# Expert stages of an attention and mixture-of-experts block: three programs merged into one, 128-row blocks, weights split once and streamed

## The reference

```python
mod = (silu(c) @ wmod).reshape(4, 6, 1, 512)           # sa, ca, ga, sb, cb, gb
h = layernorm(x) * (1 + ca) + sa
x = x + ga * attention(h)                              # 16 heads, causal, compressed keys and values
h = layernorm(x) * (1 + cb) + sb
aff = sigmoid(h @ wa)                                  # 16 experts
p, i = top_k(aff, 2); p = p / sum(p)
expert(h) = (gelu(h @ g + gb) * (h @ w1 + b1)) @ w2 + b2      # 512 -> 256 -> 512
routed = sum over the two chosen experts of p * expert(h)
shared = sum over 2 shared experts of expert(h)
out = x + gb * (h + shared + routed)
```

## Time and profile before

| | us |
|---|---|
| median of 3 timed runs | 1675.2 (1673.89 to 1675.54) |
| profiled execution | 1671.57 |
| its span, first to last instruction | 1669.7 |

### The profile page before, as it was taken

How to read it: one execution, slowest core, us unless ns; L and a number is a source line. 1 busy time by engine, 2 the same in 40 slices (tenths; PEclk the granted TensorE clock), 3 DMA queues, 4 the chain that set the end, 5 groups by cost and what they waited for, 6 DMA issues and landing times. The chain is left out here.

```text
span 1669.7 us, 26373 instructions
## 1 busy us (share of the span) xinstructions
PE 1475.5 (88%) x8146; PEld 1241.6 (74%) x8146; DVE 1006.6 (60%) x2079; ACT 613.9 (37%) x1281; POOL 491.5 (29%) x281
## 2 busy tenths in 40 slices
PE   6858892999999999989999899479994999999974
PEld 4436672888888888878888788357773999999931
DVE  3566661666668766686667766344355666666647
ACT  2332221444433434434444334121211556565510
POOL 0005574100007300380005600252001555545435
PEclk9969996999999999999999999879997999999965
DMA  9876777522242322423222420150003788889746
GB/s 305 287 207 216 218 215 251 210 70 64 69 160 80 137 75 63 157 95 125 69 76 68 157 72 30 64 196 26 26 0 99 232 288 280 286 275 281 237 146 194
DMA packets 138425, 254.91 MB, mean 153 GB/s; under 512 B 22844, under 2 KB 68832, under 8 KB 136836
## 3 DMA queue, kind: packets, MB, share of 16 engines
q1 hardware_dynamic: 123000, 191.84, 36.1%
q0 software_dynamic: 15376, 62.46, 11.1%
HBM read 186.00 MB, written 68.21 MB: 152 GB/s over the span
## 5 line engine op out<-in xcount | busy, mean ns | idle before, releaser
L897 ACT ACTIVATE a_pr<-a_pr,a_nmax 128x128 f32<-128x128 f32 (+3 forms) x256 | 142.2, 556 | 120.5 <-DVE a_nmax L949 120.0
L1631 POOL DMA_INDIRECT e_xg<-h_d,e_idx x64 | 75.7, 1183 | 274.0 <-DVE e_idx L1732 264.0
L96 PE MATMUL e_pg<-e_xT,e_w 128*128 128x256 f32 x512 | 145.2, 284 | 4.7 <-POOL e_w L1637 2.7
L97 PE MATMUL e_pg<-e_xT,e_w 128*128 128x256 f32 x512 | 144.9, 283 | 0.0
L98 PE MATMUL e_pg<-e_xT,e_w 128*128 128x256 f32 x512 | 144.7, 283 | 0.0
L949 DVE CUSTOM_DVE_ANT_0 a_pr<-a_psS,a_mask 128x128 f32<-128x128 f32 (+3 forms) x256 | 115.7, 486 | 38.2 <-PE a_psS L1027 37.1
L1039 PE MATMUL a_psY<-a_pT,a_cv 128*128 128x256 f32 (+2 forms) x768 | 134.5, 325 | 1.9 <-DVE a_pT L971 1.9
L1039 PEld LDWEIGHTS a_psY<-a_pT,a_cv 128*128 128x128 f32 x768 | 125.2, 189 | 14.6 <-issue 2.1
L96 PE MATMUL a_psX<-a_hT,a_wqk 128*128 (+1 forms) x256 | 100.7, 394 | 28.9 <-POOLq L855 28.9
L957 DVE TENSOR_SCALAR a_pr<-a_pr,a_rinv 128x128 f32<-128x128 f32 (+3 forms) x256 | 123.6, 546 | 2.2
L848 POOL DMA_DIRECT2D a_cv<-c_d x4 | 2.2, 538 | 405.2 <-PE a_psY L1039 405.2
(11 more groups left out here) (270 smaller groups left out, 3956.2 us busy)
## 6 DMA issues: line engine op xcount, KB each, us to landing
a_wqk<-wqk_d SPq DMA_DIRECT2D x64, 512.0 KB, 3.4
e_st<-in_L_ffn_rw SPq DMA_DIRECT2D x64, 512.0 KB
qpe_d<-p_qs SPq DMA_DIRECT2D x64, 256.0 KB, 4.3
a_qpe<-qpe_d SPq DMA_DIRECT2D x64, 256.0 KB, 2.6
e_st<-in_L_ffn_rg SPq DMA_DIRECT2D x32, 512.0 KB
y_d<-e_yo SPq DMA_DIRECT2D x32, 512.0 KB, 6.4
wqk_d<-w_hl SPq DMA_DIRECT2D x16, 512.0 KB, 5.4
hT_d<-p_hT SPq DMA_DIRECT2D x4, 2048.0 KB, 8.6
```

Source lines behind the costliest of these rows:

```text
L96: nc.tensor.matmul(out, sh, mh, start=n == 0, stop=False)
L97: nc.tensor.matmul(out, sh, ml, start=False, stop=False)
L897: nc.scalar.activation(pr[i], pr[i], ACT.Exp, bias=nmax[:, i:i + 1], scale=-1.0, accum_out=rsum[:, i:i + 1]).then_inc(ex, 1)
L1631: pool.indirect_dma_start(out=xg[:, u, i], out_offset=None, in_=K.h2_d, in_offset=bass.IndirectOffsetOnAxis(ap=idx[:, u, i:i + 1], axis=0) ...
```

## The change

**Blocks.** `PB` is 128 instead of 256, and there are 47 blocks instead of 32. In a block the rows are the stationary operand and the weights move: gate and up of 256 columns each are one group of 12 matmuls of 128x512, the second product 6 of 128x512, and each group gets one more matmul that adds the biases, by a one-hot of the block's expert. The product y2 then has rows on partitions and is transposed twice for the second product.

**Weights.** The routed and shared experts' weights are split once, in 72 pieces, during attention: SP loads a raw piece (three DMAs, 384 KB), ScalarE copies it (`split_high`), VectorE subtracts (`split_low`), SP stores both parts to w1s_d and w2s_d. Heads 0 to 7 carry two pieces each, the others one. In the expert stage GpSimd's queue loads 2 MB + 1 MB of split weights once per expert into a ring of three slots; TensorE reads expert and slot of each block into registers.

**Rows.** h of the second norm is spread to xs_d, in the order of the places, by 32 indirect stores; blocks then load 128 rows directly. xs_d is filled with zeros (12 DMAs of GpSimd's queue, 12.3 MB) at the beginning of attention, as places without a token are read too.

**Mhl** isn't kept: `stage_weights` stores its two parts (16 x 512 KB) to mhl_d, and attention loads 1 MB of it for each pair of heads.

**One program.** `stage_shared`, `stage_routed` and `stage_combine` become `stage_ffn`, with no barrier inside. Its order on TensorE: shared experts of sequences 0, 1, 2, then the 47 blocks, then the shared experts of sequence 3. The gathers and the combination run beside that last sequence. The sums of sequences 0 to 2 go through sum_d.

The diff, cut to its core (lines of a deleted function stand only where the text needs them):

```diff
-PB = 2 * P
-NBLK = (B * S * TOP) // PB + E
+PB = P
+NBLK = (B * S * TOP - E) // PB + E
...
 # stage_weights
-                        nc.scalar.activation(Mhl[:, bass.ds(h, 1), 0, :].rearrange("p a n -> p (a n)"),
-                                             pm[:, u % 2], ACT.Copy).then_inc(hi_w, 1)
+                        nc.scalar.activation(ml[:, u, 0], pm[:, u % 2], ACT.Copy).then_inc(hi_w, 1)
...
+                        sp.dma_start(K.mhl_d[bass.ds(j * (NI // 2) + u // 2, 1), :, u % 2].rearrange("a p s n -> (a p) s n"),
+                                     ml[:, u].bitcast(F32)).then_inc(out_s[u], 16)
...
 # SecondNorm.prepare
+        self.chain.after(nc.gpsimd.memset(self.h[:, :, :], 0.0))
+        for r in range(0, NBLK, TB):
+            n = min(TB, NBLK - r)
+            pool.dma_start(self.K.xs_d[r * P:(r + n) * P].rearrange("(t p) n -> p t n", p=P), self.h[:, 0:n]).then_inc(self.xs_zero, 16)
...
 # stage_attention, SP
+                def load_m(n, v):
+                    sp.dma_start(mh[:, v].rearrange("p u s n -> p (u s n)").bitcast(F32),
+                                 K.mhl_d[bass.ds(n % PAIRS, 1)].rearrange("a p u s n -> (a p) (u s n)")).then_inc(mh_in[v], 16)
+                def raw(i, e, q, shared):
...
+                    for n, src in enumerate((K.ins["L0_ffn_" + g_][one, row, :], K.ins["L0_ffn_" + w_][one, row, :],
+                                             K.ins["L0_ffn_" + d_][one, f_, o:o + D // 2])):
+                        sp.dma_start(rw[:, i % 2, n * F:(n + 1) * F], src.rearrange("a p f -> (a p) f")).then_inc(raw_in[i % 2], 16)
+                def keep(b, e, q):
...
+                    sp.dma_start(K.w1s_d[one, :, q].rearrange("a p s f -> (a p) s f"),
+                                 ws[:, b, :, 0:2 * F].bitcast(F32)).then_inc(ws_out[b], 16)
+                    sp.dma_start(K.w2s_d[one, :, q // 2, :, o:o + D // 2].rearrange("a p s n -> (a p) s n"),
+                                 ws[:, b, :, 2 * F:CW].bitcast(F32)).then_inc(ws_out[b], 16)
+                def head(g, e, v, u, early, more):
+                    sp.wait_ge(qp, g + 1)
+                    if more:
+                        load_w(g + 2, u)
+                    sp.wait_ge(sc, g * 4 + 4)
+                    if more:
+                        load_q(g + 2, u)
+                    if u and early > 1:
+                        sp.wait_ge(ot, g * 2 - 5)
+                        load_m((e * 4 + v * 2) // 2, v)
...
+                        sp.wait_ge(sp_lo, g + EXTRA + 1)
+                        keep(u, e, q)
+                        if more:
+                            raw(u, e + v, (q + 2) % 4, False)
...
 # stage_attention, ScalarE: after exps(g), before q_high(g + 1); heads 0 to 7 also before o_high
+                def split_high(b, i):
+                    act.wait_ge(raw_in[b], (i // 2) * 48 + 48)
+                    act.wait_ge(ws_out[b], (i // 2) * 32 + 32)
+                    nc.scalar.activation(ws[:, b, 0], rw[:, b], ACT.Copy).then_inc(sp_hi, 1)
...
 # stage_attention, VectorE: after softmax(g), before q_low(g + 1); heads 0 to 7 also before o_low
+                def split_low(b, i):
+                    dve.wait_ge(sp_hi, i + 1)
+                    nc.vector.tensor_tensor(ws[:, b, 1], rw[:, b], ws[:, b, 0].bitcast(F32), ALU.subtract).then_inc(sp_lo, 1)
...
-def stage_shared(K, N, M):
+def stage_ffn(K, N):
...
 # GpSimd
+                def spread(b, src):
+                    for t in range(TB):
+                        for k in range(TOP):
+                            n = b * TB + t
+                            pool.indirect_dma_start(out=K.xs_d, out_offset=bass.IndirectOffsetOnAxis(ap=pos[:, k, n:n + 1], axis=0),
+                                                    in_=src[:, t], in_offset=None).then_inc(xs_out[b], 16)
...
+                def expert(e, i, s):
+                    pool.wait_ge(oo, pool.value_load(lead[0:1, bass.ds(e - 2, 1)], min_val=1, max_val=NBLK))
...
+                    pool.dma_start(ring1[:, s].rearrange("p c s n -> p (c s n)").bitcast(F32),
+                                   K.w1s_d[bass.ds(e, 1)].rearrange("a p c s n -> (a p) (c s n)")).then_inc(rw_in[s], 16)
+                    pool.dma_start(ring2[:, s].rearrange("p f s n -> p (f s n)").bitcast(F32),
+                                   K.w2s_d[bass.ds(e, 1)].rearrange("a p f s n -> (a p) (f s n)")).then_inc(rw_in[s], 16)
+                    pool.wait_ge(rw_in[s], i * 32)
+                    pool.sem_inc(landed, 1)
...
 # VectorE, ahead of the third sequence's update
+                for b in range(B):
+                    dve.wait_ge(xs_out[b], 16 * TB * TOP)
...
 # TensorE
+                def gated(k, u, e, s):
+                    pe.wait_ge(landed, e)
+                    pe.wait_ge(x_lo, k + 1)
+                    w = lambda c, i: ring1[:, bass.ds(s, 1), c, i].rearrange("p a n -> p (a n)")
+                    for c in range(DC):
+                        nc.tensor.matmul(pg[:, u % 2, 0], xT[:, u % 2, 0, c], w(c, 0), start=c == 0, stop=False)
...
+                def step(j, u):
+                    k = j * XS + u
+                    e, s = expert(k), place(k)
+                    old = place(k - 1) if past(j, u, 1) else None
+                    if left(j, u, 1):
+                        trans(k + 1, j + (u + 1) // XS, (u + 1) % XS)
+                    gated(k, u, e, s)
+                    if past(j, u, 3):
+                        pe.wait_ge(yo_ok, k - 2)
+                    if past(j, u, 1):
+                        out(k - 1, (u + 3) % XS, old)
+                    pe.wait_ge(em, k + 1)
+                    for f in range(FC):
+                        m = nc.tensor.transpose(py[:, f * PB:(f + 1) * PB], y2[:, u % 2, f * P:(f + 1) * P], K.ident[:, :])
+                    m.then_inc(et, 1)
```

More of the change, by code:

```diff
@@ new lines, in _ @@
+                for t in range(TB):
+                    update(1, t)
+                    if t == 2:
+                        bases()
+                    elif t == 3:
+                        places()
+                for m in range(NU):
+                    times(2, m)
+                    y_low(2, m)
+                    if m == 0:
+                        shares()
+                    elif m == 1:
+                        tables()
+                for b in range(B):
+                    dve.wait_ge(xs_out[b], 16 * TB * TOP)
@@ new lines, in order @@
+                def order():
+                    pe.wait_ge(mb_ok, 1)
+                    pe.wait_ge(zero, 1)
+                    pe.wait_ge(aff_ok, B)
+                    nc.tensor.matmul(pr, tri[:, :], mb[:, :, :].rearrange("p t e -> p (t e)"), start=True, stop=False)
+                    for t in range(NT - 1):
+                        nc.tensor.matmul(pr[:, (t + 1) * E:].rearrange("p (t e) -> p t e", e=E), ones[:, :],
+                                         mb[:, t:t + 1].broadcast_to([P, NT - 1 - t, E]), start=False, stop=t == NT - 2)
+                    for t in range(NT):
+                        r = nc.tensor.matmul(pn, ones[:, :], mb[:, t], start=t == 0, stop=t == NT - 1)
+                    r.then_inc(ranks, 1)
@@ L1953 @@
[L1953 to L1964 removed]
+                router(0)
@@ new lines, in _ @@
+                for m in range(NU):
+                    first_(1, m, 0, gate)
+                    first_(1, m, 1, up)
+                    if m == 0:
+                        router(LAST)
+                    elif m == 1:
+                        by_token(LAST)
+                for t in range(TB):
+                    second(1, t)
+                    if t == 1:
+                        order()
+                for m in range(NU):
+                    first_(2, m, 0, gate)
+                    first_(2, m, 1, up)
@@ new lines, in _ @@
+                for t in range(TB):
+                    second(2, t)
+                    if t == 2:
+                        pe.wait_ge(tab_ok, 1)
+                        trans(0, 0, 0)
+                pe.wait_ge(bs_ok, 1)
+                pe.wait_ge(y_ok, LAST * NU)
+                pe.wait_ge(so_ok, LAST * TB)
+                pe.sem_inc(step_e, 1)
+                blocks(pe, step)
+                end = place(NBLK - 1)
+                pe.wait_ge(yo_ok, NBLK - 2)
+                out(NBLK - 1, (NBLK - 1) % XS, end)
@@ L1967, in program @@
+                for m in range(NU):
+                    first_(LAST, m, 0, gate)
+                    first_(LAST, m, 1, up)
+                for t in range(TB):
+                    second(LAST, t)
 def program(nc, ins, out):
```

1332 lines of the change are left out of this document (623 added, 709 removed).

## The result

The changed kernel takes 1731.3 us (median of 4, 1728.6 to 1732.2), the kernel before 1674.6 (4 runs): ratio 1.034, 95% interval 1.032 to 1.036. The forecast was 1641 with a range of 1580 to 1705, and 0.77 on faster. The profiled executions span 1727.0 and 1669.7 us.

What follows compares the result with a forecast made beforehand. TensorE was busy 88% of the span, with DMA full in the weight products. 1671.6 - 84 (stages after attention) + 14 + 3 + 25 + 8 = 1637.6, with the median 3.6 above: 1641 us, range 1580 to 1705.

Steps and rivals of the forecast that it cites:

- Routed block, 6.1 us: Routed experts on TensorE: 5.33 us of matmuls and transposes plus 0.8 of exposed register loads; 47 blocks, 287 us.
- Rival (b): Routed blocks: register loads and dependent addresses also expose the handovers, 7.5 us a block, 1707 us, slower than before; chance 0.14.
- First block: Attention's end to the first routed block: shared batches, then 32 indirect stores at 1.35 us each; 171 us.
- Behind the last block, 59 us: Last block to the end: last rows stored (5 us), 32 gathers (43), 11 from the last gather's issue.
- Ring, 14 us a load: Expert weights on GpSimd's queue: 3 MB an expert in 14 us, keeping up with 15 us an expert.
- Weights +14, start +3: Weight products: storing Mhl on full queues, +14 us (0 to 25); attention's start: 2.9 MB more beside hT, +3 (0 to 7).
- Transfers +25 (0 to 45): Attention's heads 0 to 7: 45 MB at 360 GB/s take 125 us, 31 more than TensorE needs; +25 us taken.
- Split beside GpSimd +8 (0 to 30): Attention heads beside GpSimd's second norm: VectorE's subtraction is slowed, 0.9 us in three heads of each of three batches.
- Split elsewhere 0: Other attention heads: the split's copy and subtraction lie where ScalarE and VectorE are idle; TensorE loses nothing, by 0.1 us a head.

Runs made afterwards that it cites:

- regs: The changed kernel with TensorE's register loads for the next block made before the wait for y2 and its transposes: 1672.0 us.
- no_low: The changed kernel without VectorE's split subtraction from head 8 on, copy, transfers and waits kept: 1694.6 us; run again in another job as no_low_b, 1719.9 us.

## Why the prediction was wrong, point by point

- **Routed block, 6.1 us.** The failing step, in two terms: the sum was 5.33 + 0.8, and what was measured is 5.2 + 0.76 + 1.27 = 7.23. First, the exposed register loads. The forecast took 1.5 us for three loads and 0.7 us of TensorE's work beside them. In the typical block the first load starts at 1460.8 and the transposes behind the loads at 1462.92, 2.1 us later, for besides the 0.30 and 0.15 us of each load and its arithmetic there are gaps between them; the work beside them lasts until about 1461.94 (the second pair of transposes, from 1461.67, takes 0.27 as in regs). So 1.0 us is exposed; the recorded idle time of 0.81 agreed with the forecast by luck, as both of its parts were too small and recorded durations are longer than distances. The longer fourth blocks and two stretches at the lower clock make it 1.27 in the mean. Second, two of the 20 wide products were costed at 0.233 us each though they contract 64 rows: they cost 0.38 more each (5.96 - 5.20 = 0.76). The Trainium skill says that changing the tiling mode drains TensorE (TensorEngine Tiling (Array Packing), Key Properties); the rows fit that, 0.32 and 0.43 us at the change against 0.22 and 0.23 without.
- **Rival (b)**, 7.5 us a block and 1707, was the nearest: the place was right, and its threshold, 6.9 us a block, was passed. It had 0.14. Its size was near in part by luck: of the 1.1 us above 6.1 only 0.5 are loads, and the handovers alone expose nothing (in regs TensorE is busy for all of 1320:1560); the rest are the 64-row products, which it didn't have. The argument against it, that a second product is always queued, was true and too weak: of that product only about 1 us was left when the loads began.
- **First block**: 171 us after attention's end, measured 173.5. Stores cost 1.27 us each (1.35).
- **Behind the last block, 59 us**: 62 from the last product in no_low, where no signal is late; 82 here. The gathers take 41 of them, as against 43; from the last gather's issue to the end it is 32 us here and 12.7 in no_low, where the forecast had 11. That signals can be late was not in any row before.
- **Ring, 14 us a load**: right (13.7 to 14.7), and hidden until a block takes 5.2 us.
- **Weights +14, start +3**: 5.4 together. Stores filled gaps: 371 GB/s at a share of 1.02, against 333 at 0.99 in the earlier trace rows.
- **Transfers +25 (0 to 45)**: 41. The mechanism and the bound were right. The sum for full queues gave 31, and I took 25, for a faster rate or for GpSimd's transfers yielding; neither came. Of the other 10 us 5 are the first heads before (89 us and not 94) and 5 the 130 us for 125. That turns go by packets decided which queue waited; that it didn't decide how long all of it took is argued from the full engines (0.98) and not tested, as no run changed the size of the packets.
- **Split beside GpSimd +8 (0 to 30)**: 16. One subtraction in each batch waits for a whole operation of GpSimd's, 5 us, and not 0.9 in each of three heads.
- **Split elsewhere 0**: right, 11.7 us a head from head 7 on.

Of the 91 us between forecast and result (spans, 1727.0 against 1635.7) the blocks hold 55, the end 23, the way to the first block 2, and what stands ahead of the routed and shared stages 11.

## What to carry to other kernels

Count what TensorE's own sequencer must do between two waits, and put register loads before a wait rather than behind it: here the same three loads cost 58 us in one place and nothing in the other. Shortening an engine's work pays only where that engine sets the pace: 13 us for the bias product alone, 32 once the loads were moved. When two queues are full, add up the bytes of both, set the time for them against what the same heads took before, and move bulk transfers to a stage with room; the size of the packets tells which queue is held back meanwhile.

## What was not expected of the hardware

- A product over 64 rows between products over 128 costs 0.38 us more than one over 128 rows that are half zeros.
- In 300:340 two full queues shared the DMA engines by packets (3093 to 2850), so 11.95 MB against 4.15.
- TensorE's signals reached VectorE, ScalarE and SyncE up to 28 us late (in no_low_b) beside indirect transfers, on three chips of five, with the same kernel on either kind (1694.6 and 1719.9 us); why is open.
- After a wait of 2.2 us TensorE's products were 0.43 us apart for 3 us, with the granted clock at the lower of its two levels, 0.50 of 2.4 GHz: a wait that cost 2.4 us cost 1.6 more behind it. In the changed kernel the same came behind two of eight idle times of 1.4 to 1.5 us; in regs, which has none in 1320:1560, it never came there.
